# Attention weights of layer 1 turned and split in the router's block, and two experts' weights loaded there

## What is computed

```python
x = x + _L0_attn_ref(_layernorm(x, axis=-1), ...)          # linear + softmax attention, gated
x = x + _L0_xattn_ref(ctx_512, _layernorm(x, axis=-1), ...)  # top-k similarity graph over the context
x = x + _L0_ffn_ref(_layernorm(x, axis=-1), ...)           # router, 32 experts of 256 slots, 8 choices a token
x = x + _L1_attn_ref(_layernorm(x, axis=-1), L1_attn_w_q, L1_attn_w_k, L1_attn_w_v, L1_attn_w_o)
x = x + _L1_xattn_ref(...)
x = x + _L1_ffn_ref(...)                                   # Walsh-Hadamard transform inside
```

## Time and profile before

| | |
|---|---|
| time, median of 3 runs | 3126.85 us (3123.44 to 3128.61) |
| profiled execution | 3120.07 us, its span 3118.0 us |
| busy share of the span | PE 79%, DVE 59%, ACT 40%, POOL 27% |
| mean granted TensorE clock | 0.886 of full speed |

### The profile page before, as it was taken

How to read it: one execution, slowest core, us unless ns; L and a number is a source line. 1 busy time by engine, 2 the same in 40 slices (tenths; PEclk the granted TensorE clock), 3 DMA queues, 4 the chain that set the end, 5 groups by cost and what they waited for, 6 DMA issues and landing times. The chain is left out here.

```text
span 3118.0 us, 34900 instructions
## 1 busy us (share of the span) xinstructions
PE 2474.1 (79%) x12662; PEld 1641.7 (53%) x12662; DVE 1844.8 (59%) x2916; ACT 1240.6 (40%) x1869; POOL 849.6 (27%) x1197
## 2 busy tenths in 40 slices
PE   5899989863532342999727999999999969999999
PEld 4454545321211122999624445545555537888887
DVE  4666665628977851777556777566555525444443
ACT  2343434328645531666411434334333313333332
POOL 1222222215567754333252343000111110000000
PEclk8899999975665565999858999999999978999999
DMA  2313132227222133899676656333433314001000
GB/s 92 85 42 82 42 82 45 68 86 283 73 68 80 52 96 121 283 305 302 213 206 158 153 155 160 92 95 91 119 97 88 99 52 178 14 28 41 1 28 14
DMA packets 200953, 340.40 MB, mean 109 GB/s; under 512 B 28810, under 2 KB 60426, under 8 KB 198755
## 3 DMA queue, kind: packets, MB, share of 16 engines
q1 hardware_dynamic: 177250, 299.80, 31.9%
q0 software_dynamic: 20480, 37.87, 4.7%
q10 hardware_dynamic: 3072, 0.79, 0.1%
HBM read 182.30 MB, written 109.05 MB: 93 GB/s over the span
## 5 line engine op out<-in xcount | busy, mean ns | idle before, releaser
L739 DVE TENSOR_REDUCE at_negmax<-at_ps 128x2 f32<-128x1024 f32 (+3 forms) x256 | 259.1, 1016 | 116.1 <-PE at_ps L505 59.4
L652 ACT ACTIVATE at_probs<-at_ps 128x1024 f32<-128x1024 f32 (+3 forms) x256 | 221.7, 866 | 265.4 <-PE at_ps L520 262.2
L1320 DVE TENSOR_REDUCE a_negmax<-a_ps 128x2 f32<-128x1024 f32 x128 | 155.2, 1217 | 134.0 <-PE a_ps L1060 133.3
L1816 ACT ACTIVATE gr_act_signs<-gr_signed,gr_test 128x512 bf16<-128x512 f32 x248 | 177.3, 716 | 133.2 <-POOL gr_test L2122 102.0
L59 PE MATMUL ff_ps<-ff_xnT_hi,ff_s_hi 128*128 128x512 f32 x512 | 200.8, 392 | 2.7 <-DVE ff_xnT_lo L2639 2.7
L60 PE MATMUL ff_ps<-ff_xnT_lo,ff_s_hi 128*128 128x512 f32 x512 | 200.2, 391 | 0.0
L61 PE MATMUL ff_ps<-ff_xnT_hi,ff_s_lo 128*128 128x512 f32 x512 | 200.1, 391 | 0.0
L520 PE MATMUL at_ps<-at_qk 98*128 98x512 f32 (+3 forms) x512 | 171.9, 418 | 16.9 <-DMA at_qk<-at_mrow 6.6
L2671 DVE TENSOR_TENSOR ff_hid<-ff_hid,ff_ps 128x512 f32<-128x512 f32 x64 | 44.0, 688 | 238.6 <-ACT ff_hid L2614 238.6
L1206 ACT ACTIVATE a_probs<-a_ps 128x1024 f32<-128x1024 f32 x128 | 130.8, 1023 | 136.5 <-PE a_ps L1076 136.0
L500 PE MATMUL at_ps<-at_qk 96*128 96x512 f32 (+3 forms) x512 | 163.1, 382 | 19.5 <-DVE at_xnT_lo L795 8.9
(11 more groups left out here) (399 smaller groups left out, 6566.9 us busy)
## 6 DMA issues: line engine op xcount, KB each, us to landing
at_qk<-at_part SPq DMA_DIRECT2D x384, 128.0 KB
ex_raw_gu<-in_L_ffn_w_gate_up_dram SPq DMA_DIRECT2D x32, 1024.0 KB
a_qk<-a_part SPq DMA_DIRECT2D x192, 128.0 KB
slot_rows<-gr_zeros SPq DMA_DIRECT2D x16, 1024.0 KB
ex_rows<-slot_rows SPq DMA_DIRECT2D x32, 512.0 KB
ex_raw_d<-in_L_ffn_w_down_dram SPq DMA_DIRECT2D x32, 512.0 KB
out_rows<-ex_y SPq DMA_DIRECT2D x32, 512.0 KB
gr_aside_raw<-in_L_ffn_W_dram SPq DMA_DIRECT2D x48, 256.0 KB
```

The source lines that it names most:

```text
L652: act.activation(probs[:, t % 2, 2 * w:2 * w + 2, lo:S], banks(("kq", g, s), lo), ACT.Exp, scale=SCALE).then_inc(free(("kq", g, s)), 1)
L739: dve.reduce_max(negmax[:, g % 2, :].rearrange("p (j t) -> p j t", t=NT)[:, 2 * w:2 * w + 2, t], banks(("qk", g, s), 0, width(g, t)), AX.X ...
L1320: dve.reduce_max(negmax[:, g % 2, :].rearrange("p (j t) -> p j t", t=NT)[:, 2 * w:2 * w + 2, t], banks(("qk", g, s)), AX.X, negate=True).t ...
L1816: act.activation(act_signs[:, j, :], src, ACT.Sign, scale=-1.0, bias=against, accum_out=total[:, i, j:j + 1]).then_inc(counted_to[j], 1)
```

## The change

The weights of the attention (their high and low parts, and w_o) get buffers that live from the router on. Their four raw loads go to buffers of the router that are done with: w_q to `zeros`, w_k to `adjacent`, w_v to `signed`, w_o to `xo`. PE, ACT and DVE turn and split them at the end of their lists in the router's block, in PSUM banks 4 to 7. The experts' raw buffers are allocated ahead of the router too, as `first_gu` (the router's `sim` lies in it) and `first_d` (`xs`), and SP loads the weights of experts 0 and 1 there behind the last adjacency; the experts' block signals them as there. `KEPT` falls from 4 to 3. The attention's first block holds only the sums of sequence 0, and `at_xs` is the first load in it.

```diff
@@ attention_layers
-        load_weights(nc, env, f"{tag}_w", [(wq, *wqT), (wk, *wkT), (wv, *wvT), (wo, woT, None)], also=lambda sp: load(sp, 0),
-                     sp_end=store_first, pool_aside=gather_first, dve_aside=add_first)
+        first_sums = nc.Block()
+        with first_sums as block:
+            @block.sync
+            def _(sp):
+                load(sp, 0)
+                for t in range(NT):
+                    store_sum(sp, 0, t)
+
+            @block.gpsimd
+            def _(pool):
+                for j in range(UNITS_B):
+                    gather(pool, 0, j)
+
+            @block.vector
+            def _(dve):
+                for j in range(UNITS_B):
+                    add_rows(dve, 0, j)
@@ graph_and_router
-        RAWS, KEPT = 4, 4
+        RAWS, KEPT = 4, 3
...
+        late_raw = [zeros[:].rearrange("p (t d) -> p t d", t=NT), adjacent[:], signed[:].rearrange("p u j s -> p (u j) s"), xo[:]]
+        LATE_BANKS = (4, 5, 6, 7)
+        late_units = [(j, c) for j in range(len(late_jobs)) for c in range(NC)]
...
+                if b == B - 1:
+                    sp.wait_ge(zeroed, 16 * (ZERO_DMAS + 1))
+                    late_load(sp, 0)
                 for n in asides(b):
...
+            sp.wait_ge(adjT, NT * B)
+            late_load(sp, 1)
+            sp.wait_ge(checked, sum(COUNTED))
+            late_load(sp, 2)
+            for e in range(2):
+                sp.wait_ge(adj, NT * B)
+                sp.dma_start(first_gu[:, e], w_gate_up[e].rearrange("(c p) f -> p c f", p=P)).then_inc(first_in, 16)
+                sp.wait_ge(blended[0], NT * B)
+                sp.dma_start(first_d[:, e], w_down[e].rearrange("(c p) f -> p c f", p=P)).then_inc(first_in, 16)
+            sp.wait_ge(stored, 16 * B)
+            sp.wait_ge(xn_done, NT * B)
+            late_load(sp, 3)
             for n in asides(B):
                 aside_traffic(n)
...
+            for u, (j, c) in enumerate(late_units):
+                if c == 0:
+                    pe.wait_ge(late_in[j], 16)
+                if u >= len(LATE_BANKS):
+                    pe.wait_ge(late_done, u - len(LATE_BANKS) + 1)
+                for t in range(NT):
+                    mm = pe.transpose(late_bank(u)[:, t * P:(t + 1) * P], late_raw[j][:, t, c * P:(c + 1) * P], env.ident[:])
+                mm.then_inc(late_turned, 1)
...
+            for u, (j, c) in enumerate(late_units):
+                high, low = late_jobs[j][1:]
+                if low is None:
+                    dve.wait_ge(late_turned, u + 1)
+                    dve.tensor_copy(high[:, c, :], late_bank(u)).then_inc(late_done, 1)
+                else:
+                    dve.wait_ge(late_high, late_highs(u))
+                    dve.tensor_tensor(low[:, c, :], late_bank(u), high[:, c, :].bitcast(F32), ALU.subtract).then_inc(late_done, 1)
@@ experts
-            load(0, 0)
-            load(0, 1)
+            for u in range(2):
+                load(0, u, weights=False)
+                sp.sem_inc(w_in[u].sem, 32)
```

More of the change, by code:

```diff
@@ L129, in _ @@
                     also(sp)
[L130 to L136, removed]
         @block.tensor
@@ L1583, in graph_and_router, with late_bank, late_load, late_highs @@
         aside_ready, aside_kept = sem("aside_ready"), sem("aside_kept")
+        late_in, late_turned, late_high, late_done = [sem(f"late_in{j}") for j in range(len(late_jobs))], sem("late_turned"), sem("late_high"), sem("late_done")
+        first_in = sem("first_in")
+        late_raw = [zeros[:].rearrange("p (t d) -> p t d", t=NT), adjacent[:], signed[:].rearrange("p u j s -> p (u j) s"), xo[:]]
+        LATE_BANKS = (4, 5, 6, 7)
+        late_units = [(j, c) for j in range(len(late_jobs)) for c in range(NC)]
+        def late_bank(u):
+            return ps[:, LATE_BANKS[u % len(LATE_BANKS)], :]
+        def late_load(sp, j):
+            sp.dma_start(late_raw[j], tiles(late_jobs[j][0])).then_inc(late_in[j], 16)
+        def late_highs(u):
+            return sum(1 for j, _ in late_units[:u + 1] if late_jobs[j][2] is not None)
         def asides(b):
@@ L1883, in _ @@
                 keep_aside(n)
+            for u, (j, c) in enumerate(late_units):
+                if late_jobs[j][2] is not None:
+                    act.wait_ge(late_turned, u + 1)
+                    act.copy(late_jobs[j][1][:, c, :], late_bank(u)).then_inc(late_high, 1)
         @block.vector
@@ L2180, with experts @@
 I_DIM = 256
-def experts(nc, env, tag, slot_rows, out_rows, w_gate_up, w_down, w2T, w2_mixed):
+def experts(nc, env, tag, slot_rows, out_rows, w_gate_up, w_down, w2T, w2_mixed, raw_gu, raw_d):
     F = 2 * I_DIM // P
@@ L2237, in _, with load @@
         def _(sp):
-            def load(i, u):
+            def load(i, u, weights=True):
                 e = i * 2 + u
@@ L2241, in load @@
                 sp.dma_start(rows[:, u], rows_dram[bass.ds(e, 1)].rearrange("e p t d -> (e p) t d")).then_inc(rows_in[u].sem, 16)
+                if not weights:
+                    return
                 gu_lo_done[u].wait(sp, i, 0)
@@ L2719, in decoder @@
             weights = moe.enter_context(nc.sbuf_tensor("weights", [P, B * NT * TOPK], F32))
+            wqT, wkT, wvT = ([moe.enter_context(nc.sbuf_tensor(f"at_{n}_{part}", [P, NC, D], F32R)) for part in ("hi", "lo")] for n in ("wq", "wk", "wv"))
+            woT = moe.enter_context(nc.sbuf_tensor("at_wo", [P, NC, D], F32))
+            late_jobs = [(arg["L1_attn_w_q"], *wqT), (arg["L1_attn_w_k"], *wkT), (arg["L1_attn_w_v"], *wvT), (arg["L1_attn_w_o"], woT, None)]
+            first = moe.enter_context(ExitStack())
+            first_gu = first.enter_context(nc.sbuf_tensor("first_gu", [P, 2, NC, 2 * I_DIM], F32))
+            first_d = first.enter_context(nc.sbuf_tensor("first_d", [P, 2, I_DIM // P, D], F32))
             graph_and_router(nc, env, "gr", steps[0], steps[1], context, arg["L0_xattn_Wq"], arg["L0_xattn_Wk"],
@@ L2722, in decoder @@
                              out_rows[SLOTS:SLOTS + 1, :], slots, weights, arg["L1_ffn_W1"], arg["L1_ffn_W3"], arg["L1_ffn_W2"],
[L2723 to L2726 removed]
+                             arg["hadamard"], w13T, w2T, late_jobs, first_gu, first_d, arg["L0_ffn_w_gate_up"], arg["L0_ffn_w_down"])
+            experts(nc, env, "ex", slot_rows, out_rows[0:SLOTS, :], arg["L0_ffn_w_gate_up"], arg["L0_ffn_w_down"], w2T, w2_mixed, first_gu, first_d)
+            first.close()
+            attention_layers(nc, env, "at", steps[1], steps[3], steps[4], wqT, wkT, wvT, woT, Routed(steps[2], out_rows, slots, weights), context, arg["L1_xattn_Wq"],
                              arg["L1_xattn_Wkv_expand"], arg["L1_xattn_Wout"])
```

32 lines of the change are left out of this document (7 added, 25 removed).

## The result

The changed kernel takes 3114.38 us (median of 10 runs, 3108.34 to 3122.95) beside 3130.64 us for the kernel before on the same chip (10 runs, 3121.97 to 3137.38). The ratio is 0.9947, with a 95% interval of 0.9934 to 0.9960: 16.3 us faster. Measured a second time on another occasion, beside 11 runs of the kernel before at 3129.32, it was 3113.51 us: ratio 0.9949 (0.9935 to 0.9963).

What follows compares the result with a forecast made beforehand. Bounds: PE inside the experts, the weight-split chain at their head, DVE's backlog at the attention's head with gather landings close behind. 13.3 + 5.8 = 19.1 us, from 3126.85 to 3107.7 us; range 3101 to 3117, own range 3104 to 3111.

Steps and rivals of the forecast that it cites:

- Attention's head: Start of the attention: weight work and 4 MB of loads leave, sums of sequence 0 end at 1602 instead of 1615.33, 13.3 us.
- the second rate: Sequence 0's gathers in the attention: after the first 4.93 MB, the other 3.46 MB go at 163 GB/s, 21 us.
- a rate other than 163 GB/s for an unseen reason: Sign of being wrong: gathers alone run faster or slower than 163 GB/s for a reason not seen.
- Rival 1: Attention's gathers keep the pace of issue: 17.8 us there, 23.6 us in all, 3103.2 us; chance 0.14.
- DVE's "backlog": Attention's start, kernel before: weights' low parts between DVE's adds make it late; this, not a landing, sets the end at 1615.33.
- Experts' head: Start of the experts: ACT splits weights already there, PE's second turn starts at 1227.2 instead of 1232.98, 5.8 us.
- Router's end: Behind the last router: 16 added weight units, some 16 us, end near 1187, hidden by POOL's scatters until 1211.7; 0 us.
- Eight loads: SP's queue in the router: early weight loads, seven of them 6.3 MB in 21 us; 0 us, up to 3 if engines are disturbed.
- `KEPT` 3: Router's asides: an ACT copy waits for the store three ago instead of four; 0 us.
- Rival 2: Attention's gathers bound from the first at 160 GB/s: 11.9 us in all, 3115; chance 0.18 including what lies towards the forecast.
- Rival 3: Router's end: DVE's new work holds up POOL's last scatters, stage 24 us later, 3132, a third 3116; chance 0.06, part or whole.
- Rival 4: Router's end: loads wait behind POOL's scatters and become its last work, net 18 us slower, 3145; chance 0.02.

## Why the prediction was right, step by step

- **Forecast.** 3107.7 us was given from 3126.85, a gain of 19.1. Measured were 16.3 and 15.8, each with some 4 us of uncertainty either way; the distances give 12.3 + 5.5 = 17.8, and the 1.5 to 2 us between are within that uncertainty. The mechanism is the forecast's: DVE follows the landings, ACT splits at once. The 3114.4 us lie inside the range and above the forecast's own 3104 to 3111. Of that, 3.8 us are the baseline, whose median was 3130.64 beside it and 3126.85 in the runs that I had.
- **Attention's head, 13.3 us.** Mis-sized by about 1 us, measured 12.3 (11.9 in the profiled pair). The end was to come 1602 - 1551.5 = 50.5 us after the first gather and came after 51.3 on average. Two errors met there and nearly cancelled, which is luck. "POOL issues 32 gathers in 40.6 us" did not survive the change: with DVE's adds beside all of it the issue took 43.6 us, and the last landing came 6.9 us after its issue, not 9. The estimate's steps came out: 4.90 MB were down by 1579, and the other 3.49 MB took 21.7 us to the last landing, 161 GB/s. But 161 is the average with the queue's end in it; from 1581 to 1593 it was 182 GB/s, and the reason for the second rate was one that I had not seen, the empty row. The prediction itself had named that, a rate other than 163 GB/s for an unseen reason, as a sign of being wrong. Rival 1 (pace of issue) is what happens with that row spread: 47.8 us, not the 46.0 that the rival had, since the issue is slower.
- **DVE's "backlog".** It was there, and part of it was the same stretch as above: w_v's last low part waited 5.58 us for ACT, and ACT 7.13 us for PE, beside POOL's gathers. In the trace of before ACT shows

```profile
1588.12 0.58 ACT L156 CAST at_wv_hi<-at_w_ps 128x512 fp32r<-128x512 f32 x1 [4.60 <-remote]
1595.84 0.58 ACT L156 CAST at_wv_hi<-at_w_ps 128x512 fp32r<-128x512 f32 x1 [7.13 <-PE at_w_ps L145]
```

  The change moved these units from beside 32 gathers to beside 32 scatters, where their waits are covered. That this was the same effect is argued from the likeness, not tried.
- **Experts' head, 5.8 us.** Right: 5.77 to gate_up, 5.5 to the first gather over the kernels.
- **Router's end, 0 us.** Right in its price, wrong in its sizing: "the units end near 1187", 17 us after `weights`, came out as 32.6 us after it, and 20.0 to 45.5 in the other executions. The 16 us of units that the prediction added up are 10.8 to 12.3 us without POOL beside them; what it lacked was the stretch. Instead of 25 us of cover 9 were left in this execution, and none in the one at 45.5, where by that estimate one more stall would have moved the stage's end. That the 0 us held in all of them is in part luck.
- **Eight loads, 0 us, and `KEPT` 3, 0 us.** Right. The share of the DMA engines rose to 1.01 in 1139 to 1157, and from the residual's store to `weights` it is 1174.33 - 1138.68 = 35.65 us, against 35.62 before. ACT waited once for a store of an aside, 1.71 us, while PE and DVE worked on the router.

```profile
1170.83 0.59 ACT L1872 COPY gr_aside_out<-gr_ps 128x512 f32<-128x512 f32 x1 [1.71 <-DMA w13T<-gr_aside_out]
```

- **Rival 2** (160 GB/s throughout) is nearest to what happens with one row for all: 60.09 us, against the 57.7 that its 1609.2 stands for. **Rival 3** did not happen: all 32 scatters took 0.97 to 1.00 us, as the rule of the Trainium skill that stands there had it for operations with one SBUF input at most. A slower issue showed elsewhere, at the gathers, where DVE's adds read two tiles of SBUF. The mean of 971 ns that the prediction held against this rival hid it: before, 17 of the 32 gathers were issued ahead of the first add, and four of the rest took 1.08 to 1.27 us. **Rival 4** did not happen: the loads were done before the scatters began.

By the round-robin rule of the Trainium skill, "DMA: Bandwidth & Descriptors", section "Queues, rings and completion order", gathers freed of the weights' 4 MB would have kept the pace of issue. They did not: the last landed 6.9 us behind its issue. With the empty row spread it was at most 3.8 (DVE's last pair of adds at 1597.52, the gather at 1593.70). So the lag came for the most part from the row and not from sharing between queues, while the issue itself had become slower by the adds.

## What to carry to other kernels

A gather whose unused entries all point at one row pays for it in the engines' time; give each partition an empty row of its own and look at the time of a packet, not only at GB/s. Work put beside a long row of indirect DMAs is covered only if its hand-overs between engines may be several times slower than its own durations say: count them with the stretch (here 20 to 45 us for 11 us of work), not by busy time, and look at several executions. And judge a change of half a per cent by the distance between two events at its seam, since the rest of a 3 ms span moves by as much from one execution to the next.

## What the runs showed of the hardware that I had not expected

- An indirect gather of 128 rows of 2 KB takes an engine 191 ns a packet (some 3.3 KB) from distinct rows and 326 ns when all read one row; 32 gathers and their sums take 48.2 and 60.1 us.
- Hand-overs from PE to ACT and DVE that took 0.2 to 0.3 us with POOL idle took 1.4 to 5.6 us beside POOL's indirect DMAs, and up to 9.1 us in other executions, after some 9 units of good pace. With POOL idle, or its scatters left out, all 16 units had none of it.
- DVE's adds with two inputs in SBUF stretch an indirect DMA's issue on POOL from 0.95 to up to 1.46 us; the low parts, which read PSUM and one tile of SBUF, left the scatters' issue at 0.97.
- One group of eight matmuls takes one of two times, though no version touches its code. PE's row near 700 us in the kernel before

```profile
698.92 3.70 PE L1695 MATMUL gr_ps<-gr_kT,gr_qT 128*128 128x512 f32 x8 [0.68 <-ACT gr_kT L1786]
```

  and in the changed kernel

```profile
700.60 6.01 PE L1715 MATMUL gr_ps<-gr_kT,gr_qT 128*128 128x512 f32 x8 [0.68 <-ACT gr_kT L1814]
```

  The mean granted clock of 695 to 725 was 0.78 and 0.66. Of the ten profiled executions of kernels that hold the attention's part, five had the short form and five the long one (6.00 to 6.17 us), among kernels with the same code there. The two kernels that were profiled twice showed the same form both times, so what decides between the forms is open.
